# A state-space layer and a spiking layer on one core: the last tile of two more states weighed by ScalarE and added by GpSimd, four gates spread over three steps, one output product a step later

## The chip, the cores and the metric

One core of one Trainium2 chip. The metric is the device time of one execution in microseconds (us); the time before is the median of three runs. Engines are named as in the profile: PE (TensorE, its weight loads as PEld), DVE (VectorE), ACT (ScalarE), POOL (GpSimd), SP (SyncE, which issues the DMAs). They run their own instruction lists in order and meet at semaphores only.

## What is computed

The input x is 8 images of 48 x 48 pixels with 256 channels, all in float32. The first layer, added to x, is a selective state-space layer; the second is a product and a leaky integrate-and-fire neuron over the images. Cut to what matters:

```
xz = gn(x) @ W_in ;  xh, z = split(xz)                 # 512 channels each
xc = depthwise_conv3x3(xh)
dt_r, B, C = split(xc @ W_xproj)                        # 8, 16, 16
dt  = softplus(dt_r @ W_dt + b_dt) ;  dtN = dt @ W_dtN + b_dtN
for t in the 2304 pixels of an image:                   # 16 states n per channel d
    h[d,n] = exp(dt[d] * A[n]) * h[d,n] + dtN[n] * B[n] * xc[d]
    y[d]   = sum_n h[d,n] * C[n] + Dskip[d] * xc[d]
y = layernorm(y) * ln_g + ln_b
x = x + (y * silu(z)) @ W_out + b_out
x = x + lif(gn(x) @ W.T + b)                            # steps over the 8 images
```

## The kernel before

**Chunks and steps.** An image is cut into 6 chunks of 8 pixel rows (384 pixels); there are 48 chunks, `iteration(b, k)` for image b and chunk k, and all of it is written out, without loops on the chip. A chunk is 16 steps, step s for state n = s. All five engines run through the same list of chunks and steps, each with its own function `iteration`; what the order is within a step is fixed by where a line stands in it. While the main work of a chunk runs, the steps also carry work for the next chunk (PRE), the one after (PRE2) and the one before (POST: layer norm, gates, output product), and of the second layer (L1) and its input (TIN). The table `STEP_GROUPS` says in which step PE fills which of the two banks of the PSUM tile `work` (names such as xh0, cv0, z0, dn, yi0, wo0); a bank may be filled again when its last content has been read.

**A step.** For state n, ACT computes the decays exp(dt * A[n]) in two parts (`next_decay`, L727, 1024 and 512 columns; in step s it makes those of state s + 1). POOL makes the scan's input B * x (`scan_input`, L599, plus L606, which adds the carry from the chunk before, in all chunks but an image's first; in step s it is that of state s + 1; three slots of `st`). DVE scans in two halves (`scan`, L1041). In the next step PE transposes the scanned state into `ht` (L1190), three tiles of 128 pixels, and the tiles are multiplied by C[n] and added into y: tiles 0 and 1 by DVE (`accumulate`, L1017). The last, third tile is weighed by ACT (`weigh`, L756, a copy with a scale into one of two slots of `weighed`) and added by POOL (`accumulate_last`, L632). For the states in `OWN`, 10 and 11, DVE does both for the third tile in one instruction of its own (L1027), in steps 11 and 12; ACT and POOL do nothing for them.

**What else stands in steps 10 to 15.** Steps 10 and 11: PE computes z0 to z3, ACT reads them through Silu, which needs a table load before and one after (both in steps 10 and 11). POOL multiplies each with the normed y (`gate`, L641): gates 0 and 1 in step 11, 2 and 3 in step 12, after the scan input and after the add if there is one. Step 12: ACT makes the first column's decays (`first_decay`, L768, not in an image's last chunk) and the normed input of a later chunk (L850), both ahead of decay 13; PE computes dn, and DVE reads it at the step's end (L1073). Step 13: POOL first multiplies the carries (`decay_carry`, L619, not in an image's last chunk). The output product comes in two halves, wo0 in step 13 and wo1 in step 15; each waits for the gates and DVE reads it into the image at the step's end (L1080), with statistics (L1087) at the end of steps 14 and 15. The skip products yi0 and yi1 are early in steps 14 and 15: PE makes them ahead of the transposes, and ACT reads them (L712) ahead of its weighing and decay, once all four gates are done, since it writes over the y that the gates read.

Of the kernel before, what the change touches and what calls it, by code (L numbers as in the profile page):

```python
# [41 lines left out]
PRE, PRE2, POST, L1, TIN, GN1 = "pre", "pre2", "post", "l1", "tin", "gn1"  # L42
# [11 lines left out]
NBT = T * DC // 512  # L54
Y_LAG = 1
NTD = NT - 1
OWN = (10, 11,)
NWT = NS - len(OWN)
CUT = 1024
FAR = 1e30  # L60
LEAST = 1e-28

# [10 lines left out]
    10: ([], [(POST, "z0"), (POST, "z1")], []),  # L73
    11: ([], [(POST, "z2"), (POST, "z3")], []),
    12: ([], [], [(PRE, "dn")]),
    13: ([], [(PRE2, "xh0")], [(POST, "wo0")]),
    14: ([(PRE, "yi0")], [(PRE2, "xh1")], []),
    15: ([(PRE, "yi1")], [], [(POST, "wo1")]),
}

# [93 lines left out]
def vssm_lif_kernel(nc, x, w_in, conv_k, w_xproj, w_dt, b_dt, a_log, dskip, w_dtn, b_dtn, ln_g, ln_b,  # L174
                    w_out, b_out, w1, b1, out):
    ctx = ExitStack()
    with ctx:
# [349 lines left out]
        def _(pool):  # L527
# [115 lines left out]
            def iteration(b, k):  # L643
                do = does(b, k)
                q0 = b * K + k - 1
                if is_first(b) and k == K - 1:
                    build_weights()
                for s in range(NS):
                    if s == 12 and k == 4 and TIN in do:
                        scale_input(0, b + 1, b, k)  # L650
                    if "main" in do:
                        if s == NCOPY + 1 and k < K - 1:
                            decay_carry(b, k, b * (K - 1) + k, 0, NCOPY)
                        if s == 2 and k > 0:
                            decay_carry(b, k, b * (K - 1) + k - 1, NCOPY, NS)
                    if s < NS - 1 and "main" in do:
                        scan_input(b, k, s + 1, 0)
                    if s == NS - 1 and PRE in do:
                        scan_input(b, k, 0, 1)
                    if s >= Y_LAG and "main" in do:  # L660
                        accumulate_last(b, k, s - Y_LAG, 0)
                    if s < Y_LAG and POST in do:
                        accumulate_last(b, k, NS - Y_LAG + s, 1)
                    if s == Y_LAG + 1 and POST in do:
                        pool.wait_ge(s_lnact, q0 * 5 + 5)
                        g.tensor_tensor(ln_nb[:, :], ln_nm[:, :], ln_rs[:, :], ALU.mult).then_inc(s_lnp, 1)
                    if s == 11 and POST in do:
                        gate(b, k, 0)
                        gate(b, k, 1)
                    if s == 12 and POST in do:  # L670
                        gate(b, k, 2)
                        gate(b, k, 3)
                    if s == 12 and PRE2 in do:
                        zero_edges(*following(b, k))
                    if s == 3 and k == 1 and GN1 in do:

                        await_filled(pool, b, 1 - K, "b1")
                        pool.wait_ge(s_setp, 1)
                        await_filled(pool, b, L1_AT[K - 1] - K, f"l{K - 1}_1")
                        scale_input(1, b - 1, b, k)  # L680
                        g.tensor_scalar(units[:, :], units[:, :], 2.0, 1.0, ALU.mult, ALU.mult).then_inc(s_unit, 1)
                        pool.wait_ge(s_unit, b)
                        pool.wait_ge(s_gpl[1], (b - 1) * 3 + 3)
                        hold("pool", pool, b)
                        g.tensor_scalar(b1cs[:, :], b1c[:, :], units[:, 0:1], 1.0, ALU.mult, ALU.mult)
                        for h in range(CH):
                            last = g.tensor_scalar(w1s[:, h, :], w1t[:, h, :], gn_rs[1][:, h:h + 1], units[:, 0:1],
                                                   ALU.mult, ALU.mult)
                        last.then_inc(s_w1s, 1)
# [242 lines left out]
        def _(dve):  # L932
# [112 lines left out]
            def iteration(b, k):  # L1045
                do = does(b, k)
# [6 lines left out]
                for s in range(NS):  # L1053
                    for h in range(2):
                        if main:
                            scan(b, k, s, h)
                        if h == 1 and L1 in do:
                            for kc, a in L1_SLOTS.get(k, ()):
                                if a == BOTH_AT and s == a + 1:
                                    reset(b, k, kc, 1)  # L1060
                                if a == BOTH_AT and s == a:
                                    charge_and_fire(b, k, kc, 0)
                                if a != BOTH_AT and s in (a, a + 1):
                                    charge_and_fire(b, k, kc, s - a)
                        if s >= Y_LAG and main:
                            accumulate(b, k, s - Y_LAG, 0, h)
                        if s < Y_LAG and post:
                            accumulate(b, k, NS - Y_LAG + s, 1, h)
                    if main and s >= Y_LAG and s - Y_LAG in OWN:
                        accumulate_last(b, k, s - Y_LAG)  # L1070
                    if s == 12 and pre:
                        jw = await_filled(dve, b, k, "dn")
                        v.scalar_tensor_tensor(out=xp[0:NS, :], in0=work[0:NS, jw, 0:T], scalar=bn_rows[:, 0:1],  # L1073
                                               in1=xp[0:NS, :], op0=ALU.add, op1=ALU.mult).then_inc(emptied[jw], 1)
                    if s in (13, 15) and post:

                        h = (s - 13) // 2
                        jw = await_filled(dve, b, k, f"wo{h}")
                        xs = img[:, img_par(b, -1 if k == 0 else 0), h, (k - 1) % K * T:((k - 1) % K + 1) * T]
                        v.scalar_tensor_tensor(out=xs, in0=work[:, jw, 0:T], scalar=bo[:, h:h + 1],  # L1080
                                               in1=xs, op0=ALU.add, op1=ALU.add).then_inc(emptied[jw], 1)
                    if s in (14, 15) and post:

                        h, kc = s - 14, (k - 1) % K
                        await_emptied(dve, b, k, f"wo{h}")
                        hold("dve", dve, b)
                        v.bn_stats(gn_st[1][:, h, kc * 6:kc * 6 + 6],  # L1087
                                   img[:, img_par(b, -1 if k == 0 else 0), h, kc * T:(kc + 1) * T]).then_inc(s_gst[1], 1)
                    if L1 in do:
                        for kc, a in L1_SLOTS.get(k, ()):  # L1090
                            if a == BOTH_AT and s == a:
                                reset(b, k, kc, 0)
                                charge_and_fire(b, k, kc, 1)
                            if a != BOTH_AT and s in (a, a + 1):
                                reset(b, k, kc, s - a)
                    if TIN in do and k in TIN_CHUNKS and s - 1 in TIN_STEPS:
                        kc = TIN_CHUNKS[k][TIN_STEPS.index(s - 1)]
                        for h in range(CH):
                            await_emptied(dve, b, k, f"ti{kc}_{h}")
                            hold("dve", dve, b)  # L1100
                            v.bn_stats(gn_st[0][:, h, kc * 6:kc * 6 + 6],
                                       img[:, img_par(b, 1), h, kc * T:(kc + 1) * T]).then_inc(s_gst[0], 1)
                    if k == 4 and TIN in do:
                        if s == 9:
                            channel_means(0, b + 1)
                        if s == 10:
                            group_deviation(0, b + 1, b, k)
                        if s == 11:
                            group_variance(0, b, k)
                    if k == 1 and GN1 in do:  # L1110
                        if s == 0:
                            channel_means(1, b - 1)
                        if s == 1:
                            group_deviation(1, b - 1, b, k)
                        if s == 2:
                            group_variance(1, b, k)
                        if s == 4:
                            jw = await_filled(dve, b, k, "b1")
                            dve.wait_ge(s_w1s, b)
                            v.scalar_tensor_tensor(out=b1s[:, :], in0=work[:, jw, 0:CH], scalar=units[:, 0:1],  # L1120
                                                   in1=b1cs[:, :], op0=ALU.mult, op1=ALU.add).then_inc(emptied[jw], 1)
# [253 lines left out]
```

## Time and profile before

| | |
|---|---|
| median of 3 runs | 4426.24 us (4418.84 to 4433.01) |
| the profiled execution's own time | 4415.12 us |
| its span, first to last instruction | 4413.4 us |
| mean granted TensorE clock | 0.922 of full speed |

The span is what the trace's times are measured in, from 0 at the first instruction. A time in a row of the timeline is the start; then comes how long the instruction was busy. A busy time can overlap the next instruction's start on the same engine by about a tenth of a us, so what an instruction costs its engine is the distance from its start to the next one's. In square brackets stands how long the engine was idle before it and which instruction ended the wait; no bracket means no idle time worth telling.

### The profile page before, as it was taken

What the parts mean: (1) busy time and instruction counts of PE and PEld (TensorE: products, weight loads), DVE (VectorE), ACT (ScalarE), POOL (GpSimd) and SP (SyncE); (2) the same over time, 40 slices, a digit from 0 to 9 for tenths busy, and PEclk for the clock granted to TensorE, in tenths of its full rate; (3) what the DMA queues carried; (4) which work ended last, traced back from release to release, by engine and by line L of the source; (5) the groups of instructions that cost most, each with busy time, mean ns of one, the idle gap of its engine ahead of it and who ended that gap; (6) DMA issues with size and microseconds to landing.
All of it is one profiled execution on the core that took longest, in us unless ns stands there. A gap on an engine that the chain in (4) does not pass through costs nothing.

```text
span 4413.4 us, 64194 instructions
## 1 busy us (share of the span) xinstructions
PE 3540.8 (80%) x20244; PEld 2225.9 (50%) x20244; DVE 4047.4 (92%) x4017; ACT 3411.3 (77%) x5782; POOL 3843.1 (87%) x2518
## 2 busy tenths in 40 slices
PE   6787888888887788877888778887887788878876
PEld 3454555555555555545554555454554555445544
DVE  3999999999999999999999999999999999999996
ACT  4778787777877787777787777887787777878774
POOL 4999999889998899888999889988899888998894
PEclk8899999998999999999899999999999899999987
DMA  5233223322233223322232223222232223222310
GB/s 132 65 97 100 65 69 100 91 87 62 85 92 92 79 61 103 91 79 75 83 102 73 79 72 101 86 75 76 89 105 65 75 82 105 83 61 80 100 54 22
DMA packets 189295, 363.22 MB, mean 82 GB/s; under 512 B 27416, under 2 KB 164120, under 8 KB 188960
## 3 DMA queue, kind: packets, MB, share of 16 engines
q1 hardware_dynamic: 188960, 359.12, 27.7%
q8 instruction: 166, 2.72, 0.3%
q14 instruction: 169, 1.38, 0.1%
HBM read 289.84 MB, written 69.21 MB: 81 GB/s over the span
## 4 chain that ended last, share of the span: by engine, by line
DVE 26%; ACT 23%; PE 20%; issue 18%; POOL 12%; DVEq 0%; DMA 0%; POOLq 0%; ACTq 0%; SPq 0%
DVE st L1041 18%; POOL st L599 10%; PE ht L1190 8%; ACT decay L727 6%; DVE y L1017 3%; ACT L918 3%; ACT weighed L756 3%; PE work L1227 2%; ACT dt L799 2%; ACT L799 2%; PE work L1262 2%; PE work L1232 1%; PE work L1163 1%; ACT xb L878 1%; PE work L1222 1%
## 5 line engine op out<-in xcount | busy, mean ns | idle before, releaser
L1041 DVE TENSOR_TENSOR_SCAN st<-decay,st 128x1024 f32<-128x1024 f32 (+1 forms) x1536 | 2731.6, 1778 | 138.6 <-ACT decay L727 101.0
L599 POOL TENSOR_TENSOR st<-xc,bbc 128x1536 f32<-128x1536 f32 x768 | 2652.0, 3453 | 56.1 <-DMA bbc<-brow 46.9
L727 ACT ACTIVATE decay<-dt,neg_a 128x1024 f32<-128x1024 f32 (+1 forms) x1536 | 1356.8, 900 | 413.4 <-DVE st L1041 410.7
L1190 PE MATMUL ht<-ident,st 128*128 128x128 f32 x9216 | 1348.5, 297 | 337.1 <-DVE st L1041 299.9
L1190 PEld LDWEIGHTS ht<-ident,st 128*128 128x128 f32 x9216 | 1134.6, 153 | 648.8 <-DVE st L1041 465.1
L1017 DVE SCALAR_TENSOR_TENSOR y<-ht,ct,y 128x512 f32<-128x512 f32 x1536 | 1119.9, 729 | 89.8 <-PE ht L1190 89.4
L632 POOL TENSOR_TENSOR y<-y,weighed 128x512 f32<-128x512 f32 x672 | 854.4, 1271 | 340.3 <-ACT weighed L756 336.1
L756 ACT ACTIVATE weighed<-ht,ct 128x512 f32<-128x512 f32 x672 | 459.4, 684 | 274.1 <-PE ht L1190 271.7
L1227 PE MATMUL work<-xn,win 128*128 128x384 f32 x768 | 344.6, 594 | 136.7 <-DVE volt L997 103.2
L1163 PE MATMUL work<-tri,conv_w 96*32 96x384 f32 x4608 | 415.6, 493 | 5.2 <-issue 2.0
L1222 PE MATMUL work<-xn,win 128*128 128x480 f32 x768 | 359.9, 593 | 4.6 <-ACT xn L850 3.2
L1227 PEld LDWEIGHTS work<-xn,win 128*128 128x128 f32 x768 | 164.9, 231 | 258.7 <-DVE volt L997 119.4
L1262 PE MATMUL work<-xb,wo 128*128 128x384 f32 x768 | 267.5, 492 | 1.6 <-ACT xb L712 1.5
L918 ACT ACT_TABLE_LOAD x192 | 246.3, 1283 | 3.4
L1163 PEld LDWEIGHTS work<-tri,conv_w 96*32 96x32 f32 x4608 | 130.7, 109 | 197.8 <-issue 188.2
L641 POOL TENSOR_TENSOR xb<-xb,y 128x384 f32<-128x384 f32 x192 | 189.0, 1001 | 43.6 <-ACT xb L712 43.1
L1222 PEld LDWEIGHTS work<-xn,win 128*128 128x128 f32 x768 | 146.4, 205 | 118.7 <-issue 100.6
L1269 PEld LDWEIGHTS work<-skip_diag,xc 128*128 128x128 f32 x1152 | 148.6, 192 | 108.0 <-DVE img L1080 76.3
L1269 PE MATMUL work<-skip_diag,xc 128*128 128x128 f32 x1152 | 155.8, 278 | 44.1 <-DVE img L1080 44.0
L1262 PEld LDWEIGHTS work<-xb,wo 128*128 128x128 f32 x768 | 139.6, 192 | 83.3 <-ACT ot L712 3.0
L1282 PE MATMUL work<-img,w1s 128*128 128x384 f32 x336 | 151.9, 595 | 36.1 <-ACT dt L799 36.1
L1244 PE MATMUL work<-xp,wdt 40*128 40x384 f32 x384 | 155.2, 525 | 27.4 <-ACT dt L799 27.4
(109 smaller groups left out, 3173.2 us busy)
## 6 DMA issues: line engine op xcount, KB each, us to landing
bbc<-brow SPq DMA_DIRECT2D x192, 768.0 KB, 6.1
tri<-rows_of_xh SPq DMA_DIRECT2D x576, 200.0 KB, 3.9
rows_of_xh<-xhp SPq DMA_DIRECT2D x192, 250.0 KB, 2.4
out_dram<-ot SPq DMA_DIRECT2D x43, 384.0 KB, 4.2
xin<-in_x_dram SPq DMA_DIRECT2D x42, 384.0 KB, 3.4
st<-in_x_dram SPq DMA_DIRECT2D x6, 384.0 KB, 5.5
out_dram<-y SPq DMA_DIRECT2D x4, 384.0 KB, 2.6
brow<-xp SPq DMA_DIRECT2D x48, 24.0 KB, 1.5
```

What stands on the lines that cost most here:

```text
L599: u = g.tensor_tensor(slot, xc[:, kq % 2, :, :], bbc[:, piece_slot(kq, p), n % PIECE, :].unsqueeze(1).to_broadcast([P, DC, T]), ALU.mult)
L632: g.tensor_tensor(y[:, kq % 2, NTD, :], y[:, kq % 2, NTD, :], weighed[:, n % 2, :], ALU.add).then_inc(s_y2, 1)
L727: a.activation(flat(decay[:, :, :])[:, lo:hi], flat(dt[:, (k + ahead) % 2, :, :])[:, lo:hi], ACT.Exp, scale=neg_a[:, n:n + 1]).then_inc(s_ ...
L756: a.activation(weighed[:, n % 2, :], ht[:, NTD, :], ACT.Copy, scale=ct[:, kq % 2, NTD * NS + n:NTD * NS + n + 1]).then_inc(s_wt, 1)
L918: a.preload_act_table_set(TABLES)
L1017: v.scalar_tensor_tensor(out=y[:, kq % 2, m, :], in0=ht[:, m, :], scalar=ct[:, kq % 2, m * NS + n:m * NS + n + 1], in1=y[:, kq % 2, m, :], ...
L1041: v.tensor_tensor_scan(state[:, lo:hi], flat(decay[:, :, :])[:, lo:hi], state[:, lo:hi], 0.0 if h == 0 else state[:, lo - 1:lo], ALU.mult, ...
L1163: last = t.matmul(work[g * Q:(g + 1) * Q, i, 0:T].rearrange("p (r w) -> p r w", w=W), conv_w[:, c * NQ + g, dx, :], tri[:, c % 2, g, :, dx ...
L1190: last = t.transpose(ht[:, m, c * P:(c + 1) * P], st[:, j, c, m * P:(m + 1) * P], ident[:, :])
L1222: last = t.matmul(work[:, i, 0:HALO], win[:, h, c * P:(c + 1) * P], xn[:, (kc + 1) % 3, h, :], start=h == 0, stop=h == CH - 1)
L1227: last = t.matmul(work[:, i, 0:T], win[:, h, D + c * P:D + (c + 1) * P], xn[:, xn0, h, W:W + T], start=h == 0, stop=h == CH - 1)
L1262: last = t.matmul(work[:, i, 0:T], wo[:, c, h * P:(h + 1) * P], zs[:, c, :], start=c == 0, stop=c == DC - 1)
```

## The change

`OWN` becomes empty: the third tiles of states 10 and 11 go the way of all others, weighed by ACT in steps 11 and 12 and added by POOL in the same steps, and DVE's two own sums go. The gates, two in step 11 and two in step 12, become one in step 11, two in step 12, one in step 13. wo0 is filled one step later, in step 14, and read by DVE at that step's end, ahead of the statistics.

```diff
-OWN = (10, 11,)
+OWN = ()
 NWT = NS - len(OWN)
 CUT = 1024
+GATES = {11: (0,), 12: (1, 2), 13: (3,)}
...
     12: ([], [], [(PRE, "dn")]),
-    13: ([], [(PRE2, "xh0")], [(POST, "wo0")]),
-    14: ([(PRE, "yi0")], [(PRE2, "xh1")], []),
+    13: ([], [(PRE2, "xh0")], []),
+    14: ([(PRE, "yi0")], [(PRE2, "xh1")], [(POST, "wo0")]),
     15: ([(PRE, "yi1")], [], [(POST, "wo1")]),
...
-                    if s == 11 and POST in do:
-                        gate(b, k, 0)
-                        gate(b, k, 1)
-                    if s == 12 and POST in do:
-                        gate(b, k, 2)
-                        gate(b, k, 3)
+                    for c in GATES.get(s, ()) if POST in do else ():
+                        gate(b, k, c)
...
-                    if s in (13, 15) and post:
-
-                        h = (s - 13) // 2
+                    if s in (14, 15) and post:
+
+                        h = s - 14
                         jw = await_filled(dve, b, k, f"wo{h}")
```

On ACT, steps 11 and 12 of a chunk, from the table load that ends the read of z0 and z1 to decay 13. Before:

```order
L918 ACT_TABLE_LOAD
L727 ACTIVATE decay<-dt,neg_a 128x1024
L727 ACTIVATE decay<-dt,neg_a 128x512
L744 ACTIVATE carry<-st 128x4
L712 ACT_TABLE_LOAD
L712 ACTIVATE xb<-work 128x384 x2
L918 ACT_TABLE_LOAD
L768 ACTIVATE a<-neg_a,dt 128x16 x4
L850 ACTIVATE xn<-img,gn_nb,gn_rs 128x480 x2
L727 ACTIVATE decay<-dt,neg_a 128x1024
```

The same stretch now (line numbers are three lower):

```order
L915 ACT_TABLE_LOAD
L753 ACTIVATE weighed<-ht,ct 128x512
L724 ACTIVATE decay<-dt,neg_a 128x1024
L724 ACTIVATE decay<-dt,neg_a 128x512
L741 ACTIVATE carry<-st 128x4
L709 ACT_TABLE_LOAD
L709 ACTIVATE xb<-work 128x384 x2
L915 ACT_TABLE_LOAD
L765 ACTIVATE a<-neg_a,dt 128x16 x4
L847 ACTIVATE xn<-img,gn_nb,gn_rs 128x480 x2
L753 ACTIVATE weighed<-ht,ct 128x512
L724 ACTIVATE decay<-dt,neg_a 128x1024
```

A weighing stands ahead of decay 12 and another ahead of decay 13.

On POOL, steps 11 to 13 of a chunk, from what follows scan input 12 to scan input 15. Before:

```order
L641 TENSOR_TENSOR xb<-xb,y 128x384 x2
L599 TENSOR_TENSOR st<-xc,bbc 128x1536
L606 TENSOR_TENSOR st<-st,cs 128x4
L641 TENSOR_TENSOR xb<-xb,y 128x384 x2
L619 TENSOR_TENSOR cs<-carry,a0 128x4x12
L599 TENSOR_TENSOR st<-xc,bbc 128x1536
L606 TENSOR_TENSOR st<-st,cs 128x4
L632 TENSOR_TENSOR y<-y,weighed 128x512
L599 TENSOR_TENSOR st<-xc,bbc 128x1536
```

The same stretch now (line numbers are one higher):

```order
L633 TENSOR_TENSOR y<-y,weighed 128x512
L642 TENSOR_TENSOR xb<-xb,y 128x384
L600 TENSOR_TENSOR st<-xc,bbc 128x1536
L607 TENSOR_TENSOR st<-st,cs 128x4
L633 TENSOR_TENSOR y<-y,weighed 128x512
L642 TENSOR_TENSOR xb<-xb,y 128x384 x2
L620 TENSOR_TENSOR cs<-carry,a0 128x4x12
L600 TENSOR_TENSOR st<-xc,bbc 128x1536
L607 TENSOR_TENSOR st<-st,cs 128x4
L633 TENSOR_TENSOR y<-y,weighed 128x512
L642 TENSOR_TENSOR xb<-xb,y 128x384
L600 TENSOR_TENSOR st<-xc,bbc 128x1536
```

Ahead of scan input 13 a gate gives way to an add; ahead of scan input 14 an add is new, in front of the gates; ahead of scan input 15 a gate is new, behind the add.

On PE, steps 13 and 14 of a chunk, where L1190 is the transposes, L1262 wo0, L1222 xh0 and xh1, L1269 yi0. Before:

```order
L1190 MATMUL ht<-ident,st 128x128 x12
L1262 MATMUL work<-xb,wo 128x384 x4
L1222 MATMUL work<-xn,win 128x480 x2
L1269 MATMUL work<-skip_diag,xc 128x128 x4
L1190 MATMUL ht<-ident,st 128x128 x12
L1222 MATMUL work<-xn,win 128x480 x2
```

The same stretch now:

```order
L1187 MATMUL ht<-ident,st 128x128 x12
L1219 MATMUL work<-xn,win 128x480 x2
L1266 MATMUL work<-skip_diag,xc 128x128 x4
L1187 MATMUL ht<-ident,st 128x128 x12
L1259 MATMUL work<-xb,wo 128x384 x4
L1219 MATMUL work<-xn,win 128x480 x2
```

wo0 goes behind yi0 and behind the transposes of step 14. As the two banks are filled in turns, yi0 now follows dn in its bank and not wo0, and yi1 follows wo0 and not yi0.

## Rows read from the trace of the kernel before

**Rows 1.** The page, part 1: busy us (share of the span), instructions.

```profile
PE 3540.8 (80%) x20244; PEld 2225.9 (50%) x20244; DVE 4047.4 (92%) x4017; ACT 3411.3 (77%) x5782; POOL 3843.1 (87%) x2518
```

**Rows 2.** Groups on POOL: count, busy us, mean ns, idle before, what ended it.

```profile
L632 POOL TENSOR_TENSOR y<-y,weighed 128x512 f32<-128x512 f32 x672 | 854.4, 1271 | 340.3 <-ACT weighed L756 336.1 <-issue 0.3
...
L619 POOL TENSOR_TENSOR cs<-carry,a 128x48 f32<-128x48 f32 x80 | 20.4, 255 | 9.0 <-ACT a L768 8.8
```

**Rows 3.** Timeline of ACT, image 1, chunk 5, decay 11 to decay 13.

```profile
1102.56 0.69 ACT L727 ACTIVATE decay<-dt,neg_a 128x512 f32<-128x512 f32 x1 [0.72 <-DVE st L1041]
1103.27 1.28 ACT L712 ACT_TABLE_LOAD   x1
...
1106.75 1.73 ACT L727 ACTIVATE decay<-dt,neg_a 128x1024 f32<-128x1024 f32 x2
...
1111.98 1.47 ACT L850 ACTIVATE xn<-img,gn_nb,gn_rs 128x480 f32<-128x480 f32 x2
1113.35 1.71 ACT L727 ACTIVATE decay<-dt,neg_a 128x1024 f32<-128x1024 f32 x2
```

**Rows 4.** Timeline of DVE, same chunk: an own sum, then scans 12 to 15 and 0.

```profile
1107.76 0.74 DVE L1027 SCALAR_TENSOR_TENSOR y<-ht,ct,y 128x512 f32<-128x512 f32 x1
1108.41 2.28 DVE L1041 TENSOR_TENSOR_SCAN st<-decay,st 128x1024 f32<-128x1024 f32 x1
...
1114.48 2.29 DVE L1041 TENSOR_TENSOR_SCAN st<-decay,st 128x1024 f32<-128x1024 f32 x1
...
1119.69 2.28 DVE L1041 TENSOR_TENSOR_SCAN st<-decay,st 128x1024 f32<-128x1024 f32 x1
...
1124.83 2.27 DVE L1041 TENSOR_TENSOR_SCAN st<-decay,st 128x1024 f32<-128x1024 f32 x1
...
1130.61 2.27 DVE L1041 TENSOR_TENSOR_SCAN st<-decay,st 128x1024 f32<-128x1024 f32 x1
```

**Rows 5.** Timeline of POOL, same chunk: scan input 13, two gates, scan input 14.

```profile
1109.23 3.44 POOL L599 TENSOR_TENSOR st<-xc,bbc 128x1536 f32<-128x1536 f32 x1
...
1112.91 1.98 POOL L641 TENSOR_TENSOR xb<-xb,y 128x384 f32<-128x384 f32 x2
1114.84 3.44 POOL L599 TENSOR_TENSOR st<-xc,bbc 128x1536 f32<-128x1536 f32 x1
```

**Rows 6.** Timeline, image 1, chunk 3: a weighing, the next decay, the add that waits.

```profile
916.49 0.69 ACT L756 ACTIVATE weighed<-ht,ct 128x512 f32<-128x512 f32 x1
917.07 1.72 ACT L727 ACTIVATE decay<-dt,neg_a 128x1024 f32<-128x1024 f32 x2
...
917.32 1.27 POOL L632 TENSOR_TENSOR y<-y,weighed 128x512 f32<-128x512 f32 x1 [1.17 <-ACT weighed L756]
```

**Rows 7.** Timeline, image 1, chunk 5: scan input 7 and its scan.

```profile
1078.33 3.44 POOL L599 TENSOR_TENSOR st<-xc,bbc 128x1536 f32<-128x1536 f32 x1
...
1082.16 2.29 DVE L1041 TENSOR_TENSOR_SCAN st<-decay,st 128x1024 f32<-128x1024 f32 x1
```

**Rows 8.** Timeline of DVE: scan 13 in the second chunk and the 46th.

```profile
227.48 2.29 DVE L1041 TENSOR_TENSOR_SCAN st<-decay,st 128x1024 f32<-128x1024 f32 x1 [1.19 <-ACT decay L727]
...
4167.71 2.29 DVE L1041 TENSOR_TENSOR_SCAN st<-decay,st 128x1024 f32<-128x1024 f32 x1 [0.44 <-ACT decay L727]
```

**Rows 9.** Timeline of DVE, image 1, chunk 0: scans 14 and 15.

```profile
663.50 2.28 DVE L1041 TENSOR_TENSOR_SCAN st<-decay,st 128x1024 f32<-128x1024 f32 x1
...
669.34 2.29 DVE L1041 TENSOR_TENSOR_SCAN st<-decay,st 128x1024 f32<-128x1024 f32 x1 [0.44 <-ACT decay L727]
```

**Rows 10.** Timeline of POOL, image 1: add 1 of chunk 4 and of chunk 5.

```profile
970.78 1.28 POOL L632 TENSOR_TENSOR y<-y,weighed 128x512 f32<-128x512 f32 x1 [2.04 <-ACT weighed L756]
...
1062.12 1.28 POOL L632 TENSOR_TENSOR y<-y,weighed 128x512 f32<-128x512 f32 x1 [0.40 <-ACT weighed L756]
```

**Rows 11.** Timeline of ACT, image 1, chunk 5, step 14: yi0, the first column.

```profile
1121.08 0.60 ACT L712 ACTIVATE y<-work 128x512 f32<-128x512 f32 x1 [1.26 <-PE work L1269]
1121.58 0.20 ACT L736 ACTIVATE dt<-far 128x4 f32<-128x4 f32 x1
```

## The prediction

> **What bounds the kernel now.** The page's first part comes first: DVE is busy 92% of the span, POOL 87%, ACT 77% [rows 1]. That looks like a kernel bound by DVE, but a share is a mean over sixteen different steps, so the next view is the order of time in the steps that the change touches. I use chunk 5 of image 1 as the example and call scan s the first half (L1041, 128x1024) of state s, D13 the start of the first part of decay 13.
>
> On ACT [rows 3] the reader should look for brackets and find them only before 1103.27. Decay 11's second part starts at 1102.56, released by DVE's scan; from there to decay 13 at 1113.35 the engine never stops: table load, z0 and z1, table load, decay 12, table load, z2 and z3, table load, the two halves of xn, decay 13. That is 10.8 us without a gap, and its start hangs on scan 10, ahead of everything the change touches. On DVE [rows 4] scan 13 starts at 1114.48, 1.13 us after D13, which is when the first part of decay 13 is written. So scan 13 starts when ACT lets it. The same holds in 45 of the 48 chunks (scan 13 within 0.05 us of the end of that decay part); the first and the last of these are [rows 8], where DVE stood idle for 1.19 and 0.44 us waiting for it. In chunks 1 to 4 the unbroken stretch starts later, at the read of z1, but ends in the same place.
>
> POOL, third, is close to its own limit: a scan input, with its carry's add, takes 3.68 us to the next instruction (1109.23 to 1112.91) [rows 5], a plain add 1.27 [rows 2], 4.95 together. DVE's steps 13, 14 and 15 take 5.21, 5.14 and 5.78 [rows 4]; step 15 has one read (wo1) more than step 14, so a read is worth 0.64 and step 13 without its own (wo0) 4.57, less than POOL needs. Steps 11 and 12, in which it has no add, are where it gets ahead.
>
> **The change, part by part.**
>
> *DVE's two own sums go.* Each holds the engine 0.65 us (1107.76 to 1108.41) [rows 4], so 1.30 per chunk, 62 us over 48 chunks. They stand in steps 11 and 12, whose end is scan 13, and scan 13 waits for ACT. I count them as worth nothing: the cover is the wait for decay 13. Were that wait not there, the 62 us would be the gain.
>
> *ACT gets two weighings.* A weighing lasts 0.69 us but the next instruction starts 0.58 after it (916.49 to 917.07) [rows 6]. Weighing 10 comes before decay 12, weighing 11 before decay 13, both inside the unbroken stretch; their inputs (transposes of states 10 and 11) are done by then or very nearly. So scan 13 is 2 x 0.58 = **1.16 us later**.
>
> *POOL gets two adds, and one of them waits.* POOL runs its queue in order. In step 12 add 11 now stands between scan input 13 and gates 1 and 2, and it waits for weighing 11, which ACT reaches only just before D13. Queued behind that wait: gates 1 and 2, in chunks 0 to 4 the carry product (L619), then scan input 14. From D13: the add starts 0.25 later (917.07 to 917.32) [rows 6]; the add 1.27 [rows 2]; two gates 1.93 (1112.91 to 1114.84) [rows 5]; the carry product 0.26 [rows 2]; and from the start of a scan input to a scan that waits for it 3.83 (1078.33 to 1082.16, in a stretch where POOL is the limit) [rows 7]. Chunk 5: 0.25 + 1.27 + 1.93 + 3.83 = 7.28; the others 7.54. Less the 1.13 from D13 to scan 13, the step from scan 13 to scan 14 takes 6.15 or 6.41 where it takes 5.21 [rows 4]: **0.94 later in chunk 5, 1.20 elsewhere**. DVE's own work in that step, now without wo0, would need only the 4.57.
>
> *One gate and one read move on.* In step 13 POOL then has scan input 14, add 12, gate 3: 3.68 + 1.27 + 0.97 = 5.92 until scan input 15 starts, and both scans hang on their inputs, so scan 14 to scan 15 takes 5.92. DVE, with wo0 moved into step 14, needs 5.78 (the step from 1124.83 to 1130.61 has the same work) [rows 4]. Now it is 5.14: **0.78 later**. In chunk 0 that step takes 5.84 already [rows 9], because the read of wo0 late in step 13 delays PE's yi0 and through it decay 15; that goes, so I count nothing there. Step 15 keeps its 5.78: POOL needs 4.95 in it.
>
> *The new wait behind gate 3.* ACT's read of yi0, early in step 14, waits for all four gates, and queued behind it are the clearing of the first column, weighing 13 and decay 15. Gate 3 ends at D13 + 3.71 + 5.92 = 9.6 (scan input 14 starts at D13 + 3.71). Then the read and the clearing (1121.08 and 1121.58, 0.7 together) [rows 11], the weighing 0.58, the decay part 1.13: ready at 12.1. Scan 15 wants it at 7.54 + 5.92 = 13.5. It hides with 1.4 us to spare; DMAs do not move against SP's other ones, and the read of dn, from which brow and bbc follow, is if anything earlier relative to scan 13.
>
> *Later chunks.* POOL starts scan input 14 4.85 us before its scan now (1114.84, 1119.69) [rows 4, 5] and 3.83 after: it stands 1 us later relative to DVE. It gets this back at add 1 of the next chunk, where it now idles 2.04 us for ACT in chunk 4; in chunk 5 the same wait is 0.40 [rows 10], so about 0.6 is passed on there, 8 x 0.6 = 5 us in all.
>
> *Sum.* Chunk 5: 1.16 + 0.94 + 0.78 = 2.88. Chunks 1 to 4: 1.16 + 1.20 + 0.78 = 3.14. Chunk 0: 1.16 + 1.20 = 2.36. An image: 2.36 + 4 x 3.14 + 2.88 = 17.8; eight: 142. Three chunks are not bound so (image 0's first has no gates; the last two have less around them): about -6. With the 5 passed on: **+141 us**. Span 4413.4 + 141 = 4554; the profiled execution's own time was 4415.12, so 4556. It stands 11 us below the median of the runs, 4426.24; 4426 + 141 = **4567**.
>
> *A rule that says otherwise.* The rows show DVE at 92% and its freed 1.30 us running into a wait. The Trainium skill, Perfetto Trace Analysis, section Optimizing Scalar/DVE Operations: "if DVE is saturated, offloading some work to Scalar (or even GPSIMD) may make sense". By that rule the sum would be 4426 less 62. The trace does not bear it out for steps 11 and 12, since DVE is not what is last there.
>
> **The rivals.**
>
> *Faster: DVE is the bound.* If ACT's stretch had 1.16 us or more to spare at scan 13, the 1.30 would come through: 4426 - 62 = 4364. For it speaks DVE's 92%; against it the 45 chunks with no slack. That is the page's rule above as a case of its own. It decides where the idle before scan 13 is not ACT's.
>
> *Only ACT's part.* If scan input 14 does not end up last, because POOL runs further ahead than I think, or ACT gives weighing 11 earlier, only 1.16 x 45 = 52 remain: 4478. For it: POOL had 4.85 us of lead at scan 14. Against it: the lead is lost at add 11, whatever came before, since POOL may not pass it.
>
> *Worse: POOL never recovers.* If the 1 us by which POOL falls behind is passed on in every chunk instead of in chunk 5 alone, it costs 40 x 1 = 40 more: 4607. For it: POOL rises by 96 x 1.27 = 122 us of work. Against it: the waits for ACT at the first adds.
>
> *No change.* The freed 1.30 and the added 1.16 nearly cancel if DVE and ACT were equally last at scan 13, and POOL kept its lead: 4426. Chunk 5, where DVE's idle time there is too short to show in the rows, is like that; the others are not, and it needs POOL's lead too.
>
> **How the numbers follow.** Forecast 0.72; only ACT's part 0.12; POOL never recovers 0.09; faster 0.04; no change 0.03. The likeliest gives 4567, by itself 4535 to 4595 (each of the three terms off by a fifth). The range takes in the rival below it and most of the one above, 4478 to 4606. A difference of 0.3%, 13 us, is about what the spread of the runs (4418.84 to 4433.01) lets one tell. All but two cases are slower by more: slower 0.93, same 0.03, faster 0.04.
>
> **What would show it.** Step 11 and 12: ACT unbroken to decay 13 with two weighings in it, scan 13 about 1.2 us later after scan 11, DVE idle before it longer by about 2.5 (1.30 + 1.16). Step 12: POOL idle before add 11, released by the weighing, and no idle after it until scan input 15; the scans' wait for POOL's st grown by some 1.5 us a chunk (6.15 or 6.41 less 4.57), 70 us in all. Scan 13 to 14 about 6.2 to 6.4, 14 to 15 about 5.9. Wrong it would be if scan 13 did not move, if POOL's add 11 found weighing 11 done, or if DVE's idle time fell.

## The result, and the profile after

| | before | after |
|---|---|---|
| median of 4 runs of each, same chip | 4426.87 us (4418.84 to 4433.01) | 4575.27 us (4572.04 to 4576.14) |
| profiled execution, own time | 4415.12 us | 4572.04 us |
| span | 4413.4 us | 4570.3 us |
| mean granted TensorE clock | 0.922 | 0.918 |

The changed kernel is slower: ratio 1.0335, 95% interval 1.0317 to 1.0353, 148 us on the medians and 157 on the two profiled executions.

The page of the kernel after, part 1 (busy us, share of the span, instructions); the row of before is in [rows 1]:

```profile
PE 3586.2 (78%) x20244; PEld 2229.1 (49%) x20244; DVE 4002.2 (88%) x3921; ACT 3464.1 (76%) x5878; POOL 3957.3 (87%) x2614
```

DVE works 45 us less and the kernel takes 157 us more. No engine is fuller than before in its share of the span; the time is in waits. The waits of the kernel after (engine, line, what it waited for: us in total, times, longest):

```profile
POOL y L633 <- ACT weighed L753: 438.3, 281, 5.5
...
DVE st L1038 <- ACT decay L724: 198.4, 194, 2.1
...
ACT y L709 <- POOL xb L642: 125.0, 46, 3.4
DVE st L1038 <- POOL st L607: 80.4, 67, 2.2
```

In the kernel before, these were 336.1 (256 times), 101.0 (137) and 14.9 (14) for the first, second and fourth; the third does not occur. DVE's scans wait 97 us more for ACT's decay and 65 us more for POOL's scan input, which was to grow by 70.

Where in a chunk the time went comes from the starts of all 768 first scan halves of each trace: the length of a step is the distance from scan s to the next, and the table sums its change from before over the 48 chunks. Where a change is given for one of the six chunks of an image, here and below, it is the mean over images 1 to 6.

| step | 0 to 10 | 11 | 12 | 13 | 14 | 15 | all |
|---|---|---|---|---|---|---|---|
| after less before, us | +13.8 | -2.3 | +62.5 | +50.7 | +30.8 | +2.3 | +157.8 |

Nine tenths are in steps 12, 13 and 14, the three that the prediction named. The same chunk as in [rows 3 to 5], image 1, chunk 5, after. ACT, from the reads of z2 and z3 to decay 13:

```profile
1144.10 0.87 ACT L709 ACTIVATE xb<-work 128x384 f32<-128x384 f32 x2
1144.99 1.28 ACT L915 ACT_TABLE_LOAD   x1
1146.28 1.46 ACT L847 ACTIVATE xn<-img,gn_nb,gn_rs 128x480 f32<-128x480 f32 x2
1147.65 0.67 ACT L753 ACTIVATE weighed<-ht,ct 128x512 f32<-128x512 f32 x1
1148.22 1.71 ACT L724 ACTIVATE decay<-dt,neg_a 128x1024 f32<-128x1024 f32 x2
```

No bracket: ACT does not stop, and weighing 11 pushes decay 13 back by 0.57 (1147.65 to 1148.22). DVE, scans 12 to 15 and the next chunk's scan 0:

```profile
1142.21 2.29 DVE L1038 TENSOR_TENSOR_SCAN st<-decay,st 128x1024 f32<-128x1024 f32 x1 [0.64 <-ACT decay L724]
...
1149.36 2.29 DVE L1038 TENSOR_TENSOR_SCAN st<-decay,st 128x1024 f32<-128x1024 f32 x1 [1.32 <-ACT decay L724]
...
1155.43 2.29 DVE L1038 TENSOR_TENSOR_SCAN st<-decay,st 128x1024 f32<-128x1024 f32 x1 [1.31 <-POOL st L607]
...
1161.65 2.29 DVE L1038 TENSOR_TENSOR_SCAN st<-decay,st 128x1024 f32<-128x1024 f32 x1 [0.33 <-issue]
...
1167.45 2.27 DVE L1038 TENSOR_TENSOR_SCAN st<-decay,st 128x1024 f32<-128x1024 f32 x1
```

Against [rows 4], the step from scan 12 takes 7.15 where it took 6.07, from scan 13 6.07 (5.21), from scan 14 6.22 (5.14), from scan 15 5.80 (5.78). The brackets show each step's last wait: ACT's decay ahead of scans 12 and 13, POOL's input ahead of scan 14. The 0.33 ahead of scan 15 has no releaser in the profile ("issue"); it is of this chunk alone, and in the other chunks 1 to 5 that step takes 5.84 to 5.90, and 6.07 in one chunk of image 0. POOL, from scan input 13 to scan input 15:

```profile
1143.50 3.43 POOL L600 TENSOR_TENSOR st<-xc,bbc 128x1536 f32<-128x1536 f32 x1
1147.01 0.21 POOL L607 TENSOR_TENSOR st<-st,cs 128x4 f32<-128x4 f32 x1
1148.46 1.27 POOL L633 TENSOR_TENSOR y<-y,weighed 128x512 f32<-128x512 f32 x1 [1.24 <-ACT weighed L753]
1149.69 1.95 POOL L642 TENSOR_TENSOR xb<-xb,y 128x384 f32<-128x384 f32 x2
1151.60 3.44 POOL L600 TENSOR_TENSOR st<-xc,bbc 128x1536 f32<-128x1536 f32 x1
...
1155.28 1.26 POOL L633 TENSOR_TENSOR y<-y,weighed 128x512 f32<-128x512 f32 x1
1156.50 1.00 POOL L642 TENSOR_TENSOR xb<-xb,y 128x384 f32<-128x384 f32 x1
1157.45 3.45 POOL L600 TENSOR_TENSOR st<-xc,bbc 128x1536 f32<-128x1536 f32 x1
```

The add at 1148.46 stands idle 1.24 us for weighing 11 and starts 0.24 after decay 13. Behind it come two gates, scan input 14, add 12, gate 3 and scan input 15 with no further idle time. The lead that POOL had at scan 14, 4.85 us in [rows 4, 5], is 3.83 (1151.60 to 1155.43).

ACT's read of yi0 does wait for gate 3, in the timeline of the same chunk:

```profile
1157.53 0.60 ACT L709 ACTIVATE y<-work 128x512 f32<-128x512 f32 x1 [2.83 <-POOL xb L642]
...
1158.12 0.68 ACT L753 ACTIVATE weighed<-ht,ct 128x512 f32<-128x512 f32 x1
1158.68 1.73 ACT L724 ACTIVATE decay<-dt,neg_a 128x1024 f32<-128x1024 f32 x2
```

Decay 15's first part is there 1.13 later, at 1159.81, and scan 15 starts at 1161.65: the wait of 2.83 costs nothing, with 1.8 to spare. Over the chunks, scan 15 starts 2.5 to 2.7 after decay 15, where it needs 1.13: 1.4 to 1.5 to spare, as forecast.

### The profile page after: what moved, and what is told of

It is laid out like the page before. It is cut to its first block, busy times and chain, and to the rows that moved or that the text cites. A ratio compares the mean times of both kernels' runs of the same rounds, so it can differ in the third digit from the quotient of the medians.

```text
span 4570.3 us, 64386 instructions
## 1 busy us (share of the span) xinstructions
PE 3586.2 (78%) x20244; PEld 2229.1 (49%) x20244; DVE 4002.2 (88%) x3921; ACT 3464.1 (76%) x5878; POOL 3957.3 (87%) x2614
## 4 chain that ended last, share of the span: by engine, by line
ACT 23%; DVE 21%; PE 19%; issue 19%; POOL 16%; SPq 1%; DVEq 0%; POOLq 0%; DMA 0%; ACTq 0%
DVE st L1038 15%; POOL st L600 11%; PE ht L1187 8%; ACT decay L724 5%; ACT L915 3%; ACT weighed L753 3%; DVE y L1014 3%; POOL xb L642 2%; ACT L796 2%; ACT dt L796 2%; PE work L1224 2%; PE work L1229 1%; PE work L1219 1%; PE work L1259 1%; POOL y L633 1%
## 5 line engine op out<-in xcount | busy, mean ns | idle before, releaser
L600 POOL TENSOR_TENSOR st<-xc,bbc 128x1536 f32<-128x1536 f32 x768 | 2651.1, 3452 | 45.1 <-DMA bbc<-brow 45.1
L1187 PE MATMUL ht<-ident,st 128*128 128x128 f32 x9216 | 1366.6, 298 | 401.4 <-DVE st L1038 329.8
L633 POOL TENSOR_TENSOR y<-y,weighed 128x512 f32<-128x512 f32 x768 | 976.6, 1272 | 441.9 <-ACT weighed L753 438.3
L753 ACT ACTIVATE weighed<-ht,ct 128x512 f32<-128x512 f32 x768 | 523.4, 681 | 265.4 <-PE ht L1187 261.9
L1259 PE MATMUL work<-xb,wo 128*128 128x384 f32 x768 | 279.6, 504 | 12.9 <-POOL xb L642 11.4
L709 ACT ACTIVATE y<-work 128x512 f32<-128x512 f32 x144 | 86.1, 598 | 199.3 <-POOL xb L642 125.0
```

The lines of the kernel that those rows point to most:

```text
L600: u = g.tensor_tensor(slot, xc[:, kq % 2, :, :], bbc[:, piece_slot(kq, p), n % PIECE, :].unsqueeze(1).to_broadcast([P, DC, T]), ALU.mult)
L633: g.tensor_tensor(y[:, kq % 2, NTD, :], y[:, kq % 2, NTD, :], weighed[:, n % 2, :], ALU.add).then_inc(s_y2, 1)
L753: a.activation(weighed[:, n % 2, :], ht[:, NTD, :], ACT.Copy, scale=ct[:, kq % 2, NTD * NS + n:NTD * NS + n + 1]).then_inc(s_wt, 1)
L1187: last = t.transpose(ht[:, m, c * P:(c + 1) * P], st[:, j, c, m * P:(m + 1) * P], ident[:, :])
L1259: last = t.matmul(work[:, i, 0:T], wo[:, c, h * P:(h + 1) * P], zs[:, c, :], start=c == 0, stop=c == DC - 1)
```

## The experiments

The theory of the prediction is that the costs are waits: two weighings in ACT's full stretch ahead of decay 13, an add in POOL's queue that waits for the second of them, and gate 3 ahead of scan input 15, with the read of wo0 moved into the same step. The main rival is that POOL has too much work now, wherever it stands. Another, that the engines slow one another down, shows nowhere in the lengths: from before to after the mean of a long scan is 2282 and 2284 ns, of a scan input 3453 and 3452, of a first decay part 1114 and 1114, of an add 1271 and 1272. All kernels compute the same output. The table sums step lengths as above, against the profiled execution of before; ratios are medians of the kernel against before on the same chip, with the 95% interval.

| kernel | time, us | ratio | 0 to 10 | 11 | 12 | 13 | 14 | 15 |
|---|---|---|---|---|---|---|---|---|
| after | 4575.27 | 1.0335 | +13.8 | -2.3 | +62.5 | +50.7 | +30.8 | +2.3 |
| 1. sums alone | 4546.26 | 1.0273 (1.0250 to 1.0295) | +24.4 | -7.3 | +62.1 | +52.1 | -2.9 | -2.9 |
| 2. gates alone | 4439.19 | 1.0032 (1.0021 to 1.0043) | +9.8 | -0.2 | +0.4 | -25.0 | +34.5 | +1.3 |
| 3. weighing 11 later | 4695.37 | 1.0608 (1.0586 to 1.0629) | +29.0 | +1.9 | +34.6 | +154.2 | +40.6 | +21.1 |
| 4. add 11 later | 4521.98 | 1.0209 (1.0165 to 1.0253) | +18.9 | -4.0 | +61.3 | -24.2 | +43.0 | -0.3 |
| 5. state 10 alone | 4463.88 | 1.0091 (1.0074 to 1.0108) | +8.1 | -6.5 | +34.6 | -22.2 | +28.6 | -2.1 |
| 6. before, xn later | 4400.10 | 0.9945 (0.9933 to 0.9956) | +14.5 | +0.5 | -28.7 | +1.4 | +1.2 | -3.2 |
| 7. add 11 and xn later | 4510.50 | 1.0196 (1.0183 to 1.0209) | +30.8 | -1.9 | +0.7 | -16.0 | +82.7 | +2.5 |
| 8. state 10, xn later | 4440.62 | 1.0032 (1.0020 to 1.0044) | +15.5 | +2.9 | -18.9 | -8.4 | +30.6 | +2.8 |
| 9. adds 10, 11 and xn later | 4463.35 | 1.0099 (1.0082 to 1.0117) | -0.9 | -3.9 | +1.7 | -18.4 | +54.5 | +10.8 |
| 10. as 9, old gates | 4475.36 | 1.0128 (1.0111 to 1.0145) | +21.3 | -7.2 | +1.1 | +23.3 | +22.0 | -2.6 |

**1. The sums alone.** The kernel before with only `OWN` emptied; gates and wo0 stay.

```diff
-OWN = (10, 11,)
+OWN = ()
```

> The kernel before with OWN empty and nothing else: the gates stay two in step 11 and two in step 12, wo0 stays in step 13. Theory 1 (two in-order queues: ACT's weighings ahead of decay 13, POOL's add 11 ahead of scan input 14, gate 3 ahead of scan input 15): the first two terms stay, 1.16 and 0.94 or 1.20 us a chunk, the third goes, since step 13 of POOL is 4.95 us again: about +106, 4533 us. Theory 2 (load: POOL's 122 us of extra work, wherever they stand, make POOL the limit): the same work as in the changed kernel, so 4575 us.

Steps 12 and 13 lengthen as in the changed kernel (62.1 and 52.1 against 62.5 and 50.7), and step 14 does not (-2.9 against +30.8). So the first two terms come with the sums, the third with the gates and the moved read, and they stand apart. The time, 4546, is 13 above the theory's 4533; step 4 alone has 20.7, which no theory named (last section).

**2. The gates alone.** The changed kernel with `OWN` as before.

```diff
-OWN = ()
+OWN = (10, 11,)
```

> The changed kernel with OWN back at (10, 11): only the gates' spread and wo0's later step are left of the change. Theory 1: POOL's lead at scan 14 is whole without the waiting add, and gate 3 in step 13 is taken out of the lead: no difference, 4427 us within 13. A rival by which the moved gate and the moved read cost by themselves, 0.78 us in 40 chunks: 4458 us. Theory 2: no added work, 4427 us.

4439 lies just inside the first theory's bounds of 13, but it is not the "no difference" that it named: the interval leaves out 1. The read of wo0 leaves step 13 (-25.0) and comes back in step 14 (+34.5), and 8 of the rest are step 4 again. Gate 3 ahead of scan input 15 costs little without add 11's wait: DVE's waits for POOL's input are 16.8 us in all, where before has 14.9.

**3. Weighing 11 behind decay 13.** One line of ACT's list in step 12 moves.

```diff
-                    if s >= Y_LAG and main:
+                    if s >= Y_LAG and main and s != 12:
                         weigh(s - Y_LAG, 0)
...
+                    if s == 12 and main:
+                        weigh(s - Y_LAG, 0)
```

> The changed kernel with one line moved on ACT: weighing 11 stands behind decay 13 and not ahead of it. ACT's stretch ahead of decay 13 is 0.58 us shorter. Theory 1: scan 13 comes only 0.58 late and not 1.16, but add 11 on POOL starts about 2.2 us later after decay 13's start, and with it gates 1 and 2 and scan input 14: about +215 against the kernel before, 4642 us, so 67 slower than the changed kernel. Theory 2 (load, or ACT's stretch alone): 4547 to 4575 us, not slower than the changed kernel.

ACT's work is the same, and so is POOL's; only the moment when add 11 may start is later. Step 12 falls to half (+34.6, one weighing), and step 13 grows by 3.1 to 3.4 us in all chunks of an image, about the 2.2 more than in the changed kernel that was forecast. If POOL's work alone counted, nothing would have been lost. The total, 4695, is 53 above the theory's: against the changed kernel, steps 14 and 15 grow by 10 and 19 and the early ones by 15, which it had left at their lengths.

**4. Add 11 behind scan input 14.** POOL's list, step 12 to step 13.

```diff
-                    if s >= Y_LAG and "main" in do:
-                        accumulate_last(b, k, s - Y_LAG, 0)
+                    if s >= Y_LAG and s != 12 and "main" in do:
+                        for n in (11, 12) if s == 13 else (s - Y_LAG,):
+                            accumulate_last(b, k, n, 0)
```

> The changed kernel with add 11 on POOL moved from step 12 to step 13, behind scan input 14 and ahead of add 12: all work is the same, but gates 1 and 2 and scan input 14 no longer queue behind the wait for weighing 11. Theory 1: only ACT's 1.16 us a chunk is left, 45 chunks: 4479 us. Theory 2 (load): 4575 us as the changed kernel.

Step 13 falls from +50.7 to -24.2, the -25 that the gates alone have: the second term is the wait, and it is gone. Step 14 ends at +43.0 instead of +31. Its change is 0.65 in chunks 1 to 3, the moved read, and 1.71 and 1.12 in chunks 4 and 5. Ahead of scan 15 DVE waits for POOL 0.97 to 0.99 us in chunk 4 of seven images and 0.22 to 0.58 in chunk 5 of six, and nowhere else. So the time comes out between the theories (the runs spread from 4494 to 4535, in the order of their granted clock, 0.935 to 0.909): the wait is shown, and POOL's work matters in the last two chunks.

**5. State 10 alone.** The changed kernel with state 11 still DVE's.

```diff
-OWN = ()
+OWN = (11,)
```

> The changed kernel with OWN = (11,): only state 10's third tile goes to ACT and POOL; state 11's stays DVE's own sum; gates and wo0 as in the changed kernel. Theory 1: weighing 10 costs ACT's stretch 0.58 us a chunk; add 10 waits for it in step 11, where POOL has a lead of several us and no scan input waits close behind: +26, 4453 us. Theory 2 (load: half the added work, half the loss): +74, 4501 us.

One weighing gives half of the first term (34.6 in step 12), and without add 11 step 13 has none of the second (-22.2). 4464 is 11 above the theory and 37 below the load.

**6. The kernel before with xn behind decay 13.** This takes ACT's 1.37 us of normed input (1111.98 to 1113.35 in [rows 3]) out of the stretch ahead of decay 13, and changes nothing else.

```diff
-                    if s == 12 and PRE2 in do:
-                        normalise_input()
...
+                    if s == 12 and PRE2 in do:
+                        normalise_input()
```

> The kernel before with one thing moved on ACT in step 12: the normed input xn (L850, 1.4 us, needed by xh0 in step 13) stands behind decay 13 and not ahead of it. Theory 1: scan 13 waits for ACT's stretch in 45 chunks, so it comes earlier by what DVE idles ahead of it, 0 to 1.2 us, about 0.5 in the mean: -22, 4405 us. If scan 13 were held by DVE's own work and not by ACT: 4427 us, no difference.

4400.10, ratio 0.9945: faster than both kernels. Step 12 shortens by 28.7 us, since the scans wait less for the decay. The row of waits of this kernel:

```profile
DVE st L1041 <- ACT decay L727: 82.7, 102, 1.4
```

In before that wait was 101.0 us, 137 times. The row holds all scans; ahead of scan 13 alone, DVE stood idle in 38 chunks, 25.3 us, before, and in none here. That ACT was last ahead of scan 13 is thus shown in the kernel before itself. Step 12 gains 0.6 us a chunk, less than the 1.37 removed: DVE is next.

**7. Add 11 and xn both later.** Experiments 4 and 6 on the changed kernel.

> The changed kernel with add 11 behind scan input 14 on POOL and xn behind decay 13 on ACT. Theory 1: ACT's stretch gains 1.37 us and has lost 1.16, so it is 0.2 us a chunk shorter than in the kernel before; DVE has 1.30 us less: 4427 - 9 = 4418 us, within noise of the kernel before. Theory 2 (load): at least 4530 us.

The theory missed by 92 us. The ACT part went as forecast (step 12 is +0.7), but step 14 rose to +82.7: 1.07 in chunk 0, 1.67 to 2.16 in the others. POOL, image 1, chunk 2, from add 10 on:

```profile
851.58 1.27 POOL L633 TENSOR_TENSOR y<-y,weighed 128x512 f32<-128x512 f32 x1 [5.24 <-ACT weighed L754]
852.81 1.00 POOL L642 TENSOR_TENSOR xb<-xb,y 128x384 f32<-128x384 f32 x1
853.77 3.44 POOL L600 TENSOR_TENSOR st<-xc,bbc 128x1536 f32<-128x1536 f32 x1
...
859.62 3.46 POOL L600 TENSOR_TENSOR st<-xc,bbc 128x1536 f32<-128x1536 f32 x1
...
863.31 2.63 POOL L633 TENSOR_TENSOR y<-y,weighed 128x512 f32<-128x512 f32 x2
865.90 1.00 POOL L642 TENSOR_TENSOR xb<-xb,y 128x384 f32<-128x384 f32 x1
866.86 3.46 POOL L600 TENSOR_TENSOR st<-xc,bbc 128x1536 f32<-128x1536 f32 x1
```

Scan 15 starts at 870.71, 3.85 after the last of these starts, which is POOL's pace [rows 7], and DVE waits 0.96 for it. Followed back, POOL has no idle time until 851.58, where it stood 5.24 us: add 10 waits for weighing 10, with gate 0 and scan input 13 queued behind it. It is the second term over again, one state earlier; in the changed kernel the longer wait of add 11 covers it.

**8. State 10 alone, xn later.**

> OWN = (11,), gates and wo0 as in the changed kernel, and xn behind decay 13 on ACT. Theory 1: ACT's stretch is 1.37 - 0.58 = 0.79 us shorter than in the kernel before, DVE has 0.65 us less, so scan 13 comes up to 0.79 earlier, less where POOL is the limit: about -30, 4397 us, faster than both kernels. Theory 2: about 4480 us.

Missed by 44, in part in the same way: there is no add 11 here, but add 10 starts at 842.68 in image 1, chunk 2, after 5.08 idle for weighing 10, and POOL is unbroken from there to scan input 14, 850.74, whose scan it holds to 854.58. That is why step 13 is -8.4 and not the -22.2 of experiment 5: 14 of the 44. The early steps have 15.5 more, and step 14 its +30.6, the moved read, which the theory left out.

**9. Adds 10 and 11 both behind, xn too.** Experiment 7 and add 10 in step 12, behind scan input 13.

```diff
-                    if s >= Y_LAG and s != 12 and "main" in do:
-                        for n in (11, 12) if s == 13 else (s - Y_LAG,):
+                    if s >= Y_LAG and "main" in do:
+                        for n in {11: (), 12: (10,), 13: (11, 12)}.get(s, (s - Y_LAG,)):
                             accumulate_last(b, k, n, 0)
```

> The run with add 11 and xn behind, and in addition add 10 moved from step 11 to step 12, behind scan input 13. Base is that run's 4510. Theory that it is waits in POOL's queue: in that run POOL stands idle 5.24 us ahead of add 10 for weighing 10 (add 10 starts at 851.58 in image 1, chunk 2) and is then unbroken until scan input 15, whose scan starts at 870.71 where DVE alone would have reached 869.75. With add 10 behind it, scan input 13 has to wait only for its slot (the transposes of state 10, done just ahead of weighing 10 at 850.75), so 1.5 to 3 us earlier; scan 15 is then DVE's, 0.96 earlier in some 46 chunks: 4510 - 44 = 4466 (4450 to 4480). Rival, that POOL has too much work in steps 11 to 15 whatever it waits for: the same work in the same steps, 4510 (4500 to 4520).

4463.35, where the theory of the waits said 4466 and the work theory 4510. But the sum is right only in part for its reason: against experiment 7, step 14 gave back 28 of the 44, the early steps 32, which neither theory named (6 in step 4, the rest spread and not taken apart), and step 15 lost 8. By chunk the reason is clearer. In chunks 1 to 3 step 14 is +0.65, the moved read and nothing more; in chunks 4 and 5 it is +2.07 and +2.13, unchanged from experiment 7. POOL there, image 1, chunk 5, from the last time that it is idle to scan input 15:

```profile
1109.57 1.27 POOL L633 TENSOR_TENSOR y<-y,weighed 128x512 f32<-128x512 f32 x1 [0.74 <-ACT weighed L754]
1110.80 3.44 POOL L600 TENSOR_TENSOR st<-xc,bbc 128x1536 f32<-128x1536 f32 x1
...
1134.39 3.45 POOL L600 TENSOR_TENSOR st<-xc,bbc 128x1536 f32<-128x1536 f32 x1
1137.92 0.21 POOL L607 TENSOR_TENSOR st<-st,cs 128x4 f32<-128x4 f32 x1
```

POOL's last stop is five steps earlier, at add 8, and scan 15 starts behind this last row, at 1138.59, DVE having waited 1.68 (0.35 of it in this image alone: in the others scan 15 follows its input at POOL's pace, 3.85). In between POOL waits for nothing: in the last two chunks of an image the rival, POOL's work, is right.

**10. As 9, with the gates and wo0 where they were before.**

> The same with the gates and wo0 as in the kernel before (gates 0 and 1 in step 11, 2 and 3 in step 12, wo0 in step 13). Theory of the waits: nothing that POOL waits for stands ahead of a scan input in steps 11 to 13, so scans 13, 14 and 15 go as DVE's work or ACT's decay lets them, which is the kernel before: steps 13 and 14 take about 5.2 and 5.1; with the moved xn paying for the two weighings, and 12 to 20 us more in the early steps as in the other runs: 4426 + 15 = 4440 (4425 to 4460). Rival, POOL's work: two adds more in these steps as in the changed kernel, 4500 or more.

4475.36, between the two. Step 14 is better than in 9 (0.23 in chunks 1 to 3; in chunks 4 and 5, where POOL is last again, 1.1 to 1.2), step 13 worse, +0.74 to +0.82 in chunks 1 to 3. DVE's last row before scan 14, image 1, chunk 2:

```profile
857.81 0.62 DVE L1078 SCALAR_TENSOR_TENSOR img<-work,bo,img 128x384 f32<-128x384 f32 x1 [0.73 <-PE work L1260]
```

It waits for wo0, and wo0 in PE's timeline waits for ACT to read `ot`:

```profile
854.92 2.85 PE L1260 MATMUL work<-xb,wo 128*128 128x384 f32 x8 [1.56 <-ACT ot L710]
```

In ACT's timeline that read stands behind the moved xn:

```profile
851.18 1.72 ACT L725 ACTIVATE decay<-dt,neg_a 128x1024 f32<-128x1024 f32 x2
852.84 1.46 ACT L848 ACTIVATE xn<-img,gn_nb,gn_rs 128x480 f32<-128x480 f32 x2
854.19 0.20 ACT L742 ACTIVATE carry<-st 128x4 f32<-128x4 f32 x1
854.29 0.85 ACT L710 ACTIVATE ot<-work 128x512 f32<-128x512 f32 x2
```

In experiment 6 the order on ACT is the same, but there decay 13 is 1.90 us ahead of its scan and not 1.14 as here (scan 13 starts at 852.32), so `ot` and wo0 come in time. The theory took the two edits as independent; the move that pays ahead of decay 13 costs behind it, once ACT is last.

## Why the prediction held

**DVE's own sums at nothing: right.** DVE's busy time fell by 45 us and its waits took it up: ahead of scan 12 it now stands idle 26.0 us in all, where it did not before, and ahead of scan 13 89.8 instead of 25.3. The Trainium skill, Perfetto Trace Analysis, section Optimizing Scalar/DVE Operations, says that offloading some work from a saturated DVE to Scalar or even GPSIMD may make sense; here DVE was 92% busy [rows 1], the offloading with the moves that came with it cost 148 us (the sums alone 121 in experiment 1), and the measurement decides.

**ACT's two weighings: right, somewhat too small.** 1.16 x 45 chunks is 52; step 12 grew by 62.5 and step 11 fell by 2.3. By chunk the two steps together grew by 1.14 in chunk 0, 1.79, 1.48 and 1.24 in chunks 1 to 3, and 1.13 and 1.15 in chunks 4 and 5. The excess in chunks 1 to 3 is an idle time that the prediction put at nothing (its inputs "are done by then or very nearly"): weighing 10 waits there for PE's transposes of state 10, 0.72, 0.35 and 0.11 us. In image 1, chunk 1, ahead of decay 12:

```profile
759.45 0.69 ACT L753 ACTIVATE weighed<-ht,ct 128x512 f32<-128x512 f32 x1 [0.62 <-PE ht L1187]
```

Chunk 4 has a wait of 0.35 too and no excess; in chunks 0 and 5 there is none. Experiments 1, 5 and 6 undo this term whole, by half, and in the kernel before.

**Add 11's wait: right.** 0.94 in chunk 5 and 1.20 elsewhere were forecast, 0.88 in chunk 5 and 0.84 to 1.23 elsewhere measured. Experiment 4 removes the wait and the term, experiment 3 lengthens both.

**Gate 3 ahead of scan input 15: right in size, but nearly all of it is the read.** 0.78 was forecast for step 14 in chunks 1 to 5 and 0.71 to 0.78 measured; chunk 0, counted at nothing, gave 0.12. The prediction let POOL set the step at 5.92, with DVE at 5.78 close behind. In the kernel after they are level: scan 15 starts 3.84 to 3.90 after its input in chunks 1 to 5, POOL's pace, but DVE shows an idle time ahead of it in two chunks only, 0.5 us in all. So gate 3 adds about 0.1 to what DVE's own work needs. Experiment 2 shows the rest: wo0's read alone adds 0.65 to step 14 and takes 0.52 from step 13. In the changed kernel POOL holds scan 14, so the 0.52 does not come back.

**What is passed on: too large, and not add 11's alone.** Of the 5 us that chunk 5 was to lose through POOL after add 1, about 2 show, 0.22 in steps 4 and 5 of each such chunk, where the scans do start at POOL's pace. Experiment 2, which has no add 11, has 0.31 there, so add 11's wait is not needed for it. The early steps lost 13.8 in all, 13.0 of them in step 4 (12.2 in chunks 2 and 3). There it goes with PE's clock (last section) and not with POOL: ahead of scan 5, DVE's wait for POOL hardly changed (13.6 and 13.9 us), and the one for ACT's decay rose from 4.1 to 10.7. The rival in which POOL never recovers did not come: the waits at the early adds gave the lead back, as expected.

**Sum.** 2.36 for chunk 0 was too much (1.80), 3.14 too little for chunks 1 to 3 (4.1 to 4.3, with 0.9 to 1.0 of it in step 4 of chunks 2 and 3), near for chunk 4 (3.06) and for chunk 5 (3.05 against 2.88). The misses add to 16 us on a sum of 141, and they are net of opposite ones: chunk 0 was 0.56 too high, chunks 1 to 3 about 1.0 too low. The median is only 8 above the forecast, because the profiled execution of the kernel after is 3 us below its median, and that of before is 11 below; that half of the miss does not show there is luck.

**What the prediction did not see** is how far its second term reaches. It read add 11's wait as one fault of one place. Experiments 7 to 9 show a row of them: take add 11's wait away and add 10's holds POOL, take that away and POOL's work from add 8 on does, in two chunks of six, while in experiment 10 wo0 is late through ACT.

## What to carry to other kernels

An operation taken from a busy engine is worth what that engine's next wait leaves of it: look first for the last wait in the steps where the operation stands, since 62 us of freed DVE time ran into waits here. On the receiving engines the operation's place in the queue costs more than its length: an add of 1.27 us that waits for ACT ahead of a scan input cost up to 1.2 us of a step, and nothing of that step behind it (step 13 in experiment 4; in an image's last two chunks step 14 then paid). What did pay, by 0.55%, was to move unhurried work behind the instruction that others wait for, as in experiment 6; experiment 10 shows the same move delaying wo0. When an experiment removes one wait, follow the queue back to the next idle time before forecasting the gain.

## What was not expected of the hardware

PE's granted clock falls for short stretches, and where it falls changes with the order of the work. Windows of the kernel before, image 1, chunk 2 (us from and to, length, busy time of PE, PEld, DVE, ACT and POOL with counts, granted clock, DMA share, GB/s):

```profile
766.20:770.20 4.00, 1.81 (x8) 0.75 (x6) 4.00 (x5) 2.12 (x3) 3.92 (x4) 1.00 0.82 251
770.30:773.70 3.40, 3.40 (x12) 2.73 (x12) 3.40 (x5) 2.73 (x8) 3.09 (x3) 0.50 0.21 75
```

And of the kernel after, same chunk:

```profile
806.80:810.80 4.00, 1.91 (x20) 0.84 (x8) 4.00 (x5) 3.35 (x7) 3.48 (x2) 1.00 0.78 251
810.90:814.30 3.40, 3.30 (x18) 2.97 (x22) 2.46 (x3) 0.92 (x3) 1.29 (x2) 0.50 0.45 145
814.40:818.40 4.00, 4.00 (x44) 2.36 (x40) 3.09 (x4) 3.71 (x8) 3.23 (x2) 1.00 0.00 0
```

The clock goes from full to 0.50, the lower of its two levels (1.2 of 2.4 GHz). Before, that was in step 1 of this chunk; after, in step 4, while PE transposes state 3 for DVE. Of the 41 chunks from image 1 on, without the last, the granted clock of step 1 is below 0.9 in 24 before and in none after, that of step 4 in 6 and in 15. In step 1 the low clock costs little: the step is 4.3 us shorter in all after, 0.25 in this chunk; step 4 is 1.50 longer here (5.21 and 6.71). That place in the timeline of before, then of after:

```profile
788.64 0.66 PE L1291 MATMUL work<-ident,ob 128*128 128x128 f32 x4 [2.03 <-ACT xc L712]
...
789.83 1.47 PE L1190 MATMUL ht<-ident,st 128*128 128x128 f32 x12
790.47 0.75 DVE L1017 SCALAR_TENSOR_TENSOR y<-ht,ct,y 128x512 f32<-128x512 f32 x1 [0.27 <-PE ht L1190]
```

```profile
810.09 0.66 PE L1288 MATMUL work<-ident,ob 128*128 128x128 f32 x4 [2.03 <-ACT xc L709]
...
811.48 2.77 PE L1187 MATMUL ht<-ident,st 128*128 128x128 f32 x12
812.58 0.75 DVE L1014 SCALAR_TENSOR_TENSOR y<-ht,ct,y 128x512 f32<-128x512 f32 x1 [0.94 <-PE ht L1187]
```

The twelve transposes take 2.77 instead of 1.47, and DVE waits 0.94 instead of 0.27. PE had been idle 2.03 us ahead of both, so an idle stretch alone does not tell where the clock falls. Step 4's change, split by its granted clock in the same 41 chunks: after, the 15 chunks below 0.9 hold 11.2 us and the others 1.1; in experiment 1 it is 20.1 in 19 chunks and 0.0 in the others; in experiment 6, 14.3 in 15, which is half of what moving xn gained in step 12; in experiment 9 only 4 chunks are low. What decides whether the clock falls in step 1 or in step 4 stays open, and no run here changed the clock by itself: that it is the cause of step 4's growth rests on the split and on the longer transposes. In the first three of these runs it is a cost of 11 to 20 us that no term of the prediction holds.
